# First attention of a vision tower: TensorE takes a unit's turns ahead of the projection and the values

## The reference

```python
def _L0_attn_ref(x, W_qkv, b_qkv, rel_bias, W_proj, b_proj):
    # H = 4 heads of HD = 16, WIN = 64, LEFT = 31, x is (4, 1025, 64), layer-normed
    qkv = (x @ W_qkv + b_qkv).reshape(n, t, 3, H, HD)
    q, k, v = (qkv[:, :, 0], qkv[:, :, 1], qkv[:, :, 2])
    idx = jnp.arange(t)[:, None] + jnp.arange(WIN)[None, :] - LEFT
    ...
    kw = k[:, idx_c]
    vw = v[:, idx_c]
    attn = jnp.einsum('nthd,ntwhd->nhtw', q * SCALE, kw)
    attn = attn + rel_bias
    attn = attn + jnp.where(valid, 0.0, MASK_VAL)[None, None]
    attn = jax.nn.softmax(attn, axis=-1)
    out = jnp.einsum('nhtw,ntwhd->nthd', attn, vw).reshape(n, t, c)
    return out @ W_proj + b_proj
```

## Time and profile before

| | us |
|---|---|
| time, median of 3 runs | 5268.02 (5265.84 to 5275.31) |
| profiled execution | 5290.05 |
| its span | 5288.4 |
| PE busy | 4373.7 (83%) |
| DVE busy | 3540.2 (67%) |
| ACT busy | 2158.2 (41%) |
| POOL busy | 968.8 (18%) |
| window stage | 180 to 341 us of the span |

### The profile page before, as it was taken

How to read it: one execution, slowest core, us unless ns; L and a number is a source line. 1 busy time by engine, 2 the same in 40 slices (tenths; PEclk the granted TensorE clock), 3 DMA queues, 4 the chain that set the end, 5 groups by cost and what they waited for, 6 DMA issues and landing times. The chain is left out here.

```text
span 5288.4 us, 70724 instructions
## 1 busy us (share of the span) xinstructions
PE 4373.7 (83%) x24566; PEld 2659.6 (50%) x24566; DVE 3540.2 (67%) x8758; ACT 2158.2 (41%) x3709; POOL 968.8 (18%) x1114
## 2 busy tenths in 40 slices
PE   7666999999999998999999799999499999961004
PEld 3442444444444444444455455555388889851002
DVE  7665777777777776767655688887655556774325
ACT  1452444444444444444444455555133343320002
POOL 0132111111111111111000100000333310005771
PEclk9875999999999999999999899999599999975556
DMA  2015355666454545574644511110200010000110
GB/s 71 9 48 99 95 134 126 134 122 139 121 140 121 140 121 123 119 129 120 142 129 111 147 37 37 33 30 1 46 8 16 7 20 6 6 2 7 21 14 12
DMA packets 324608, 389.23 MB, mean 74 GB/s; under 512 B 119821, under 2 KB 274713, under 8 KB 323456
## 3 DMA queue, kind: packets, MB, share of 16 engines
q1 hardware_dynamic: 233956, 186.63, 17.9%
q0 software_dynamic: 58224, 171.28, 10.8%
q10 hardware_dynamic: 32076, 26.80, 2.9%
HBM read 313.90 MB, written 70.64 MB: 73 GB/s over the span
## 5 line engine op out<-in xcount | busy, mean ns | idle before, releaser
L1083 PE MATMUL mem_kv<-mem_weights,mem_table 128*128 128x456 f32 x4608 | 1957.9, 546 | 0.0
L1351 DVE SCALAR_TENSOR_TENSOR mem_weights<-mem_above,mem_exps 128x912 f32<-128x912 f32 x1152 | 1273.6, 1106 | 703.1 <-ACT mem_exps L1228 700.2
L1228 ACT ACTIVATE mem_exps<-mem_above 128x912 f32<-128x912 f32 x1152 | 1069.7, 929 | 948.1 <-PE mem_above L1070 947.8
L1083 PEld LDWEIGHTS mem_kv<-mem_weights,mem_table 128*128 128x128 f32 x4608 | 872.2, 189 | 568.5 <-issue 452.7
L1070 PE MATMUL mem_above<-mem_operands,mem_selector 123*128 123x456 bf16 x2304 | 637.8, 358 | 69.7 <-DMA mem_inv_z<-scratch_inv_z 44.4
L2290 DVE TENSOR_REDUCE mha_chunk_max<-mha_max_scores 114x1 f32<-114x342 f32 x864 | 439.3, 513 | 310.3 <-PE mha_max_scores L2062 292.6
L2085 PE MATMUL mha_sums<-mha_probs,mha_value_wide 114*72 114x114 f32 (+1 forms) x5184 | 607.8, 261 | 14.2 <-ACT mha_probs L2272 14.2
L2085 PEld LDWEIGHTS mha_sums<-mha_probs,mha_value_wide 114*72 114x72 f32 (+1 forms) x5184 | 560.0, 143 | 23.2 <-issue 21.0
L1070 PEld LDWEIGHTS mem_above<-mem_operands,mem_selector 123*128 123x128 bf16 x2304 | 218.3, 98 | 588.5 <-issue 476.1
L2272 ACT ACTIVATE mha_probs<-mha_scores 114x912 f32<-114x912 f32 x324 | 297.6, 930 | 385.0 <-PE mha_scores L2074 372.4
L971 POOL DMA_DIRECT2D mem_table<-in_L_ffn_tables_dram x288 | 153.3, 538 | 1380.7 <-PE mem_kv L1083 1375.0
(11 more groups left out here) (598 smaller groups left out, 5078.6 us busy)
## 6 DMA issues: line engine op xcount, KB each, us to landing
mem_table<-in_L_ffn_tables_dram POOLq DMA_DIRECT2D x288, 512.0 KB
mem_operands<-scratch_second_scores SPq DMA_DIRECT2D x216, 256.5 KB
mem_operands<-scratch_first_scores SPq DMA_DIRECT2D x288, 128.2 KB
mem_inv_z<-scratch_inv_z SPq DMA_DIRECT2D x72, 228.0 KB
scratch_second_scores<-mem_sel_parts ACTq DMA_DIRECT2D x81, 171.0 KB
scratch_first_scores<-mem_sel_parts ACTq DMA_DIRECT2D x108, 114.0 KB
scratch_mem_q<-mem_weights SPq DMA_DIRECT2D x16, 513.0 KB, 6.7
scratch_mem_keys<-mem_kvT SPq DMA_DIRECT2D x72, 114.0 KB, 9.6
```

Of the source, the lines that this page charges most:

```text
L1083: last = nc.tensor.matmul(acc[k][:, 0:SPAN], table[:, k, ch, :], W[:, J % 3, c, :], start=(ch == 0), stop=(ch == CHUNKS - 1))
L1228: nc.scalar.activation(E[:, J % 2, :, :], psD[J % 2][:, :, 0:SPAN], ACT.Exp).then_inc(exped, 1)
L1351: nc.vector.scalar_tensor_tensor(W[:, J % 3, :, :], psD[J % 2][:, :, 0:SPAN], 0.0, E[:, J % 2, :, :], ALU.is_ge, ALU.mult).then_inc(weight ...
```

## The change

In TensorE's step the call of `flip(t - 3)` moves up, from behind `value(t - 3)` to right behind `score(t)`. All else stays: the instructions, their shapes, their semaphores, and the order on the other engines.

```diff
             for t in range(STEPS):
                 if live(t):
                     score(t)
+                if live(t - 3):
+                    flip(t - 3)
                 if live(t - 5):
                     project(t - 5)
                 if live(t - 3):
                     value(t - 3)
-                    flip(t - 3)
                 if live(t - 4):
                     attend(t - 4)
```

## The result

Before: median 5266.93 us of 4 runs (5260.80 to 5275.31). After: 5334.49 us of 4 runs (5325.41 to 5344.25). The ratio is 1.0123, with a 95% interval from 1.0111 to 1.0135: slower by 58 to 71 us by that interval, and the medians lie 67.6 us apart.

A forecast was written before the change was run, and what follows sets the result against it. A ring of TensorE and ScalarE waiting for each other bounds the loop, 3.58 us a step. At 1.2 GHz it becomes 5.84: +4.5, +71.7 over 32 steps and +5.0 make +81, so 5349 us, range 5291 to 5358.

The forecast's parts named there:

- The ring: Loop step: turns wait for ScalarE's copy, behind exponentials that wait for values; 4.36 us against 3.58 at 2.4 GHz.
- The size at the lower level: Whole loop with TensorE at 1.2 GHz: 5.84 us a step, together +81 us.
- the turns: Ring member on TensorE, the eight turns ahead of the projection: 1.72 us at 1.2 GHz, 0.93 at 2.4.
- the projection: Ring member on TensorE behind the turns: 0.50 us at 1.2 GHz, doubled from 0.25.
- the values: Ring member on TensorE, from the values until ScalarE copies them: 1.11 us at 1.2 GHz.
- the hand-over to the turns: Ring member from ScalarE's copy of turns to TensorE's next turns: copy 0.53 us and hand-over 0.06.
- The size at the upper level: Loop with TensorE at 2.4 GHz from 218.8 on: 4.36 us a step, +29 us, time 5297.
- the likelier case: TensorE's clock stays at the lower level for the whole loop: 5349 us, chance 0.50.
- an early return: Rival: TensorE's clock comes back in the loop's first few steps: 5297 to 5304 us, chance 0.32.
- The first pause: TensorE's wait in the loop's first steps, until the first copy of turns ends: over 1 us.
- comes and goes: Rival: TensorE's clock returns late or rises and falls in the loop: about 5325 us, chance 0.15.
- not slower: Rival: the turns fit into TensorE's spare 0.75 us a step, ring stays 3.58: 5268 us, chance 0.03.

The follow-up runs named there:

- e3_between: Kernel after, with the turns on TensorE moved between the projection and the values: 5360.45 us, ratio 1.0130 to the kernel before.
- e2_early_copy: Kernel after, with ScalarE's copy of the turns of unit t - 3 moved ahead of its value copies and exponentials: 5318.86 us, ratio 1.0052 to before.
- e1_fill: Kernel after, with three matmuls that compute nothing added behind each unit's scores: 5319.63 us against 5287.52 before, ratio 1.0058.
- e12: Kernel after, with ScalarE's earlier copy of turns, VectorE's reciprocal ahead of its scaling, and values ahead of the projection: 5253.35 us, ratio 0.9976 to before.
- e11: Kernel after, with ScalarE's earlier copy of turns and VectorE's reciprocal ahead of its scaling: 5255.78 us, ratio 0.9985 to before.
- e7 to e10: Kernel after with ScalarE's early copy and TensorE's scores behind the values, two with values before projection, two with earlier reciprocal: ratios 1.0178 to 1.0237 to before.
- after_again: Kernel after, unchanged, run again on another chip: 5332.52 us against 5273.52 before, ratio 1.0111.

## Why the prediction was right

**The ring: right, its members between 0.2 shorter and 0.04 longer.** It was forecast that the turns wait for ScalarE's copy, that the copy stands behind the exponentials, and that these wait for the values. The rows of after agree with each of the three, though for the first the profile names no releaser, where the prediction asked for its name. That the members add up to 5.46 proves nothing, since each is read from one start to the next. What tests the ring is the edits. e3_between shows that the turns' length ahead of the values makes the step long even with their wait hidden. e2_early_copy shows what the wait is worth: the step falls from 4.19 (e1_fill) to 3.3 at the upper level, but only from 5.46 to 5.28 at the lower. At the lower level, where the kernel after works, TensorE's own chain is nearly as long as the ring: the 0.2 of pause ahead of the turns (forecast 0.4) is all that lies between the two, and an earlier copy can save no more. ScalarE's wait for the values grew to 2.8, not to 3.2, and the stage ended at 406.9, not at 422.

**The size at the lower level: too long.** Of the forecast 5.84 the turns were 1.72 (measured 1.55), the projection 0.50 (0.30), the values 1.11 (1.06), the hand-over to the turns 0.59 (0.63). In all 5.46. The term "turns" was taken from the earlier trace rows, where the scores or the products follow behind the turns; the scores' weights, for one, load only at 213.44, 0.33 behind the start of the last turn and together with their first matmul. In the rows of after the projection's weights load at 292.50, with the last turn, and the projection starts 0.19 later. The Trainium skill, "TensorE: Matmul & The Clock Gate", section "Step-by-step: what each phase is for", says that a weight load can be pulled ahead of matmuls in flight; this trace agrees, and I had left the sum with the rows. Doubling the projection was wrong too: the end at 0.25 was nearer. 32 steps of 0.38 are 12.2 us of the 14.8 between the forecast +81 and the measured +66.2. Of the rest, 1.6 is that the clock was up three times for a short while, and 1.1 lies in the loop's two ends.

**The size at the upper level: too long as well.** Forecast 4.36 and +29 us; e1_fill measured 4.19 and +25.6. The turns took 0.81 there (265.35 to 266.16), not 0.93. That the two totals lie so close is in part luck: the first copies cost 1.3 and not 4.2, and the end, at the lower clock, 4.5 and not 0.5.

**The clock: the likelier case came, nearly pure.** It was given 0.50, against 0.32 for an early return. The first pause was forecast at over 1 us and measured 1.71; the wait between values and products at about 0.5 and measured 0.62; the one ahead of the turns at about 0.4, measured 0.2 (scores at 290.06, 0.87 long as in the earlier trace rows, turns at 291.14). The short rises belong to the rival "comes and goes", which was read as a mean of two sums; they were worth 1.6 us.

**Why it falls and rises: only half of it holds.** I argued that pauses in each step keep the clock down. e1_fill agrees, where the fill lets the clock up. But e12 worked almost without a pause from 225 to 239 at 0.50 (13.88 of 14.00), and e11 got the clock back with a pause of half a microsecond in its steps. So the branch at 0.50 came true, but the reason given for it does not decide it, and with a chance of 0.50 it was no sure call. At the upper level the clock fell within 3.4 us in after, with 1.69 of 3.20 us busy, and held in before, e1_fill and e11, with 93.7 of 120, 113.0 of 135.8 and 88.4 of 112.4. What decides the rise, in e12 and between e2 and e11, stays open.

**The rival "not slower" was out, for the named reason only at the upper level:** the copy of turns came behind the exponentials. With the copy early (e2) the step is below 3.58 at the upper level and still 5.28 at the lower. A second psT tile, which would take that wait away without moving the copy, wasn't tried.

## What to carry to other kernels

Before a block is moved up on one engine, write down for every engine what will stand behind it, and who waits for that: the ring here was closed by ScalarE's exponentials, the larger part of the price (1.27 of 1.88 us a step) came from the lower clock, and the failures of e7 to e10 by VectorE's and GpSimd's order, which I had not drawn. A new order on one engine may pay only when its partners' orders move with it: this same move cost 1.2% alone and gains 0.15% with an earlier copy on ScalarE and an earlier reciprocal on VectorE, 0.34% with the values ahead of the projection and one idle matmul besides. Whether the move has a share in those gains is not shown: the earlier reciprocal was not run with the order of before. In a loop whose granted clock can take either level, price each order at both levels, and look at the granted clock of every stretch before you believe a ratio.

## What the runs showed of the hardware that I had not expected

- The clock can rise for 3.4 us and fall again, three times in a row in after and twice in after_again, with TensorE's order of work unchanged.
- Eight f32 turns of 114 rows with the projection behind them take 1.55 us at 1.2 GHz and 0.81 at 2.4 GHz, measured from start to start.
- Three matmuls a step that nobody reads made a kernel 0.5 to 0.6% faster (ratio 1.0058 against 1.0111 and 1.0123).
- TensorE busy for 13.88 of 14.00 us at 0.50 (e12) did not get the clock back in those 14 us; it rose at 239.1, just behind them.
- Two kernels with TensorE busy for the same 6.69 of 7.20 us at 0.50 (e2 and e11, 212.0 to 219.2) got the clock back 11 us apart, at 230.2 and 219.3.
